# The head of a group-normalised convolution: pair 0 loaded in four transfers, its first upper half made in two operations, and a store placed ahead of a load

## The reference

```python
g = v.reshape(B_, G, C_ // G, H_, W_)          # G = 32 groups of two channels
m = mean(g, axis=(2, 3, 4)); s = var(g, axis=(2, 3, 4))
gn = ((g - m) / sqrt(s + 1e-5)).reshape(v.shape)
out = x + conv(gn, sign(W), padding 1)         # the forward value of the binarised weight is sign(W)
```

## Time and profile before

| | |
|---|---|
| median of 3 runs | 206.25 us (205.93 to 206.54) |
| the profiled execution, its own time | 206.47 us |
| its span | 204.7 us |
| TensorE matmul busy | 196.7 us, 96% of the span |
| weight loads, beside the matmuls | 165.3 us, 81% |
| VectorE busy | 149.0 us, 73% |
| ScalarE busy | 138.5 us, 68% |
| GpSimd busy | 134.8 us, 66% |
| HBM traffic | 25.84 MB read, 25.69 MB written, 252 GB/s over the span |

### The profile page before, as it was taken

How to read it: one execution, slowest core, us unless ns; L and a number is a source line. 1 busy time by engine, 2 the same in 40 slices (tenths; PEclk the granted TensorE clock), 3 DMA queues, 4 the chain that set the end, 5 groups by cost and what they waited for, 6 DMA issues and landing times.

```text
span 204.7 us, 10453 instructions
## 1 busy us (share of the span) xinstructions
PE 196.7 (96%) x4782; PEld 165.3 (81%) x4782; DVE 149.0 (73%) x320; ACT 138.5 (68%) x177; POOL 134.8 (66%) x86
## 2 busy tenths in 40 slices
PE   1999999999999999999999999999999999999993
PEld 0686978878899999989788787978788797878873
DVE  1894997976949496794949689594958859460955
ACT  3295969588593949769394976939496794939500
POOL 1059596939586793958578495858859585875900
PEclk9999999999999999999999999999999999999999
DMA  6949788887969788796979879697887969442464
GB/s 209 313 152 303 202 335 278 259 298 210 351 180 378 235 275 286 220 382 164 366 218 294 284 231 365 144 387 205 307 283 261 304 172 370 181 160 95 154 230 160
DMA packets 19116, 52.20 MB, mean 255 GB/s; under 512 B 2112, under 2 KB 4928, under 8 KB 19072
## 3 DMA queue, kind: packets, MB, share of 16 engines
q1 hardware_dynamic: 19072, 51.54, 74.9%
HBM read 25.84 MB, written 25.69 MB: 252 GB/s over the span
## 4 chain that ended last, share of the span: by engine, by line
PE 92%; DMA 3%; DVE 2%; SPq 1%; ACT 0%; issue 0%; DVEq 0%
PE psum L513 91%; DMA w_raw<-in_L_conv_W_dram 3%; DVE xbuf L466 2%; SPq L155 1%; PE psum L487 1%; ACT w_sign L290 0%; PE psum L497 0%; DVEq L56 0%
## 5 line engine op out<-in xcount | busy, mean ns | idle before, releaser
L236 POOL TENSOR_TENSOR los<-xnorm,his 128x840 f16<-128x840 f32 (+1 forms) x64 | 105.9, 1686 | 26.4 <-ACT his L274 15.8
L513 PE MATMUL psum<-los,w_taps 64*64 64x392 f16 (+1 forms) x2268 | 110.5, 325 | 0.0
L513 PE MATMUL psum<-his,w_taps 64*64 64x392 f16 x2268 | 110.2, 325 | 0.0
L513 PEld LDWEIGHTS psum<-his,w_taps 64*64 64x64 f16 x2268 | 81.9, 107 | 15.8 <-issue 0.4
L513 PEld LDWEIGHTS psum<-los,w_taps 64*64 64x64 f16 x2268 | 84.1, 107 | 13.0 <-POOL los L236 0.6
L388 DVE SCALAR_TENSOR_TENSOR xbuf<-psum,xbuf 128x784 f32<-128x784 f32 (+1 forms) x60 | 58.1, 969 | 40.8 <-PE psum L513 39.9
L339 DVE BATCH_NORM_STATS2 stats<-xbuf 128x6 f32<-128x448 f32 x112 | 64.0, 614 | 4.4 <-DMA xbuf<-in_x_dram 3.9
L266 ACT ACTIVATE xnorm<-xbuf,coef 128x784 f32<-128x784 f32 (+2 forms) x62 | 62.7, 1035 | 1.4 <-DVE coef L371 1.0
L274 ACT CAST his<-xnorm 128x784 f16<-128x784 f32 (+2 forms) x62 | 50.2, 835 | 0.3 <-issue 0.2
L242 POOL TENSOR_TENSOR xbuf<-moved,xbuf 128x784 f32<-128x784 f32 x15 | 27.9, 1863 | 32.9 <-ACT moved L283 32.9
L282 ACT ACTIVATE moved<-psum 64x784 f32<-64x784 f32 x15 | 12.3, 820 | 44.2 <-PE psum L513 44.2
(11 more groups left out here) (26 smaller groups left out, 21.8 us busy)
## 6 DMA issues: line engine op xcount, KB each, us to landing
out_dram<-xbuf SPq DMA_DIRECT2D x63, 392.0 KB, 4.7
xbuf<-in_x_dram SPq DMA_DIRECT2D x47, 448.0 KB, 4.4
xbuf<-in_x_dram SPq DMA_DIRECT2D x18, 224.0 KB, 4.9
out_dram<-xbuf SPq DMA_DIRECT2D x1, 224.0 KB, 2.2
out_dram<-xbuf SPq DMA_DIRECT2D x2, 84.0 KB, 1.8
w_raw<-in_L_conv_W_dram SPq DMA_DIRECT2D x1, 144.0 KB, 5.3
```

The costliest lines, as they stand in the source:

```text
L236: nc.gpsimd.tensor_tensor(rows(los[:, pair % HRING, :], a, b), rows(xnorm[:, pair % NRING, :], a, b), rows(his[:, pair % HRING, :], a, b), ...
L513: mm = pe.matmul(outs[:, a - n * BR:b - n * BR, left:right], w_taps[lanes, t, :], rows(half[lanes, slot, :], a + dy, b + dy)[:, :, left + ...
```

## The change

Pair 0 is loaded in four transfers of one, two, two and two of its seven pieces, in place of five of two, two, one, one, one. Its first upper part (15 rows) is made in two operations of 8 and 7 rows, each raising hi_first, and GpSimd's first los waits for both. In the first phase of pair 0 the taps of block 0 (the first two matmuls of a pass) run two taps ahead of those of block 1: after two half passes of block 0 alone TensorE waits for the second operation, goes on with both blocks, and ends with two half passes of block 1 alone. In SyncE's loop the store of a pair's first half stands ahead of the load that waits for the pair's fourth phase.

```diff
@@ -44,7 +44,7 @@
     SN = 8 * W
     NS = HW // SN
     PARTS = [range(0, 2), range(2, 4), range(4, 6), range(6, NS)]
-    PARTS0 = [range(0, 2), range(2, 4), range(4, 5), range(5, 6), range(6, NS)]
+    PARTS0 = [range(0, 1), range(1, 3), range(3, 5), range(5, NS)]
     assert PAIRS % XRING == 0 and (PAIRS - 1) % HRING == 0
 
 
@@ -191,8 +191,8 @@
             for phases in range(1, 4):
                 load_after(phases)
             for pair in range(PAIRS - 1):
+                store(pair, 0)
                 load_after(4 * pair + 4)
-                store(pair, 0)
                 load_after(4 * pair + 5)
                 store(pair, 1)
                 load_after(4 * pair + 6)
@@ -230,7 +230,7 @@
                 if pair == 0 and c < 2:
                     pool.wait_ge(xnorm_first, c + 1)
                 if pair == 0 and c == 0:
-                    pool.wait_ge(hi_first, 1)
+                    pool.wait_ge(hi_first, 2)
                 else:
                     pool.wait_ge(hi_ready, hi_done(pair, c))
                 nc.gpsimd.tensor_tensor(rows(los[:, pair % HRING, :], a, b), rows(xnorm[:, pair % NRING, :], a, b),
@@ -376,11 +376,12 @@
                 nc.vector.tensor_scalar(xnorm[:, 0, a * W:b * W], xbuf[:, 0, a * W:b * W],
                                         coef[:, 0, 0:1], coef[:, 0, 1:2], ALU.mult, ALU.add).then_inc(xnorm_first, 1)
 
+
             def hi_of_first():
-                a, b = CHUNKS[0]
                 dve.wait_ge(coef_ready, 1)
-                nc.vector.tensor_scalar(his[:, 0, a * W:b * W], xbuf[:, 0, a * W:b * W],
-                                        group[:, 0:1], coef[:, 0, 0:1], ALU.subtract, ALU.mult).then_inc(hi_first, 1)
+                for a, b in ((0, BR + 1), (BR + 1, CUTS[1])):
+                    nc.vector.tensor_scalar(his[:, 0, a * W:b * W], xbuf[:, 0, a * W:b * W],
+                                            group[:, 0:1], coef[:, 0, 0:1], ALU.subtract, ALU.mult).then_inc(hi_first, 1)
 
 
             def evacuate(pair, g, lanes, of, odd, done):
@@ -503,11 +504,12 @@
 
             ORDER = [4, 0, 2, 6, 8, 1, 3, 5, 7]
 
-            def products(slot, half, g, k, t, start, stop):
+            def products(slot, half, g, k, t, start, stop, parities=(0, 1)):
                 dy, dx = t // KW - 1, t % KW - 1
                 left, right = max(0, -dx), min(W, W - dx)
                 n0 = 4 * g + 2 * k
-                for lanes, cols, n in ((LOW, LOW, n0), (HIGH, HIGH, n0), (LOW, HIGH, n0 + 1), (HIGH, LOW, n0 + 1)):
+                tiles = ((LOW, LOW, n0), (HIGH, HIGH, n0), (LOW, HIGH, n0 + 1), (HIGH, LOW, n0 + 1))
+                for lanes, cols, n in tiles[2 * parities[0]:2 * parities[-1] + 2]:
                     a, b = max(n * BR, -dy), min((n + 1) * BR, H - dy)
                     outs = psum[cols, bank_of(n), 0:BN].rearrange("p (h w) -> p h w", w=W)
                     mm = pe.matmul(outs[:, a - n * BR:b - n * BR, left:right], w_taps[lanes, t, :],
@@ -551,10 +553,16 @@
                     if pair == 0 and g == 0:
 
                         pe.wait_ge(hi_first, 1)
-                        for i, t in enumerate(ORDER):
-                            if t == 1:
-                                pe.wait_ge(w_ready, 2)
-                            products(slot, his, 0, 0, t, i == 0, False)
+
+                        for i in range(TAPS + 2):
+                            if i < TAPS:
+                                if ORDER[i] == 1:
+                                    pe.wait_ge(w_ready, 2)
+                                products(slot, his, 0, 0, ORDER[i], i == 0, False, (0,))
+                            if i == 2:
+                                pe.wait_ge(hi_first, 2)
+                            if i >= 2:
+                                products(slot, his, 0, 0, ORDER[i - 2], i == 2, False, (1,))
                         pe.wait_ge(hi_ready, hi_done(0, 1))
                         phase(slot, 0, 1)
                         pe.wait_ge(lo_ready, lo_done(0, 0))
```

## The result

The changed kernel takes 208.3 us (median of 20 runs, 206.70 to 210.09) against 206.17 us (20 runs, 205.59 to 206.84) before: 2.1 us longer. The median lies outside the range that was given (205.7 to 207.6 us). Its direction is the one that was forecast, its size three times as large (2.1 against 0.65 us).

A forecast was written before the change was run, and what follows sets the result against it. TensorE's one long piece of 186.89 us was taken to bound the kernel, so only its start counts. Later statistics, the split and half passes, partly hidden, summed to +0.67 us: 206.25 + 0.67 = 206.9 us, range 205.7 to 207.6.

The forecast's parts named there:

- What bounds the kernel: One piece of 186.89 us of TensorE work; only how early the first block begins and whether it runs without holes counts.
- Term 1: VectorE's statistics of pair 0 end later, two pieces behind the last landing: +0.58 us, bounds -0.05 and +0.9 us.
- Term 2: The earlier first half of the upper part does not start TensorE's convolution sooner: no gain.
- Term 3: Splitting the first upper half in two operations delays the bias, normalised piece and GpSimd: +0.09 us, ends 0 and 0.15.
- The passes: Half passes of two matmuls lengthen the first 18 his passes on TensorE: +0.17 us, from a range of 0.17 to 0.33.
- Term 4: In SyncE's loop, putting the store ahead of the load does not hold the load: 0.
- rival D: TensorE's clock still low at the convolution's start after the pause behind the warm-up: 208 us, at most 208.7; chance 6%.
- A: The forecast itself, the start of the convolution block shifted later: 206.9 us, own range 206.6 to 207.3; chance 55%.

The follow-up runs named there:

- e1: The kernel before with only the four transfers of one, two, two and two pieces: 209.15 us, ratio 1.0135.
- e4: The changed kernel with 18 warm-up rounds in place of 14 ahead of the first transposes: 207.82 us, ratio 1.0075.
- e9: The changed kernel with its warm-up spread over the four landings and 9 rounds between the transposes in place of 6: 207.85 us, ratio 1.0063.
- e2: The kernel before with only the upper half in two operations and block 0 two taps ahead: 206.32 us, ratio 1.0008.
- e14: The changed kernel with pair 0 in six transfers of one, two, one, one, one, one piece and the warm-up spread over them: 206.27 us, ratio 0.9985.
- e3: The kernel before with only the store moved ahead of the load: 205.97 us, ratio 0.9999.
- e7: The changed kernel with 9 warm-up rounds between the two transposes in place of 6: 208.25 us, ratio 1.0075.
- e6: The changed kernel with the warm-up waiting for pair 0's second landing in place of the first: 207.84 us, ratio 1.0075.
- e8: The changed kernel with 18 warm-up rounds ahead of the first transposes and 9 between the transposes, in place of 14 and 6: 207.40 us, ratio 1.0056.
- e15: The kernel before with seven transfers of one piece, the warm-up spread over them and the store ahead of the load: 207.30 us, ratio 1.0036.
- e5: The kernel before with 10 warm-up rounds ahead of the first transposes in place of 14: 206.62 us, ratio 1.0007.
- e11: The kernel before with 10 warm-up rounds ahead of the first transposes and 3 between the transposes, in place of 14 and 6: 207.54 us, ratio 1.0055.
- e12: The kernel before with pair 0 in four transfers of two, two, two and one piece: 207.19 us, ratio 1.0014.

## Why the prediction was wrong

- **What bounds the kernel**: right. The long piece was 187.14 us after and 186.89 before; all that changed lies ahead of 17 us.
- **Term 1, statistics, +0.58 us**: in the profiled execution +0.35 us. The last landing came at 7.93 us and not 8.1, and two statistics took 1.15 us. Its mechanism stood in every profile with the four transfers, but its size scatters: the last statistics end at 9.1 us (after), 9.6 (e1), 9.4 (e4), 10.7 (e9) against 8.75 before. The bound of +0.9 us was too near: in e9 it is +2.0. I took the third landing as fixed by the bytes it closes; with two pieces in it, it came between 6.1 and 8.5 us. This is the second step that failed.
- **Term 2, the earlier half brings nothing**: right. It was there at 10.98 + 0.51 = 11.5 us, and TensorE's first weight load came at 11.61 us, right behind the last round. That load moved by 0.15 us only, though the deviation moved by 0.35: the copy behind it had waited for the first transposes as well, and came 0.20 us later (10.14 against 9.94 us). I had allowed it 0.05 us of slack.
- **Term 3, +0.09 us**: measured +0.19 us (0.82 against 0.63 us from start to start). The slope between 784 and 840 columns was carried too far: 448 and 392 columns take 0.514 and 0.479 us. Here the 0.16 us by the Trainium skill's fixed term (VectorE: DVE Perf Modes, the TRN2 errata) was the better number.
- **The passes, +0.17 us**: both his phases take 3.48 us from their first matmul where they took 3.18 in the same view, +0.30 us, close to the upper end of two passes; in e2 it is +0.15 us (3.33 us), in e14 +0.22 us. It costs next to nothing here, as GpSimd's piece is ready at the same time (12.85 + 2.17 = 15.02 us); e2 as a whole is at +0.1 us.
- **Term 4, the store, 0**: right. The two stores are issued from 22.28 us in place of 24.32, now ahead of the third load, which follows at 24.42 us; it was at 23.87 us, and moved as all of TensorE's work did (+0.55 us), so it is not held. e3's ratio is 0.9999.

```profile
18.44 3.32 SPq L165 DMA_DIRECT2D xbuf<-in_x_dram  x2
22.28 0.82 SPq L184 DMA_DIRECT2D out_dram<-xbuf  x2
```

- **The step that failed is rival D**, which the sum of 206.9 us put at nothing. Its mechanism was the one that decided, and its place was named: the pause between warm-up and transposes. It got 6%, and 13 of 20 runs have a low clock. Two readings were wrong in it. I let the warm-up start at 3.8 us and end at 8.6 us; it started at 3.40 us and was over at 7.94 us, so the idle time was 1.48 us and not the 0.7 us until 9.3 us. And I took the later shift of 0.5 us in ScalarE's chain for a shift only, when it opened a second idle stretch on TensorE of 0.49 us. The Trainium skill (TensorE: Matmul & The Clock Gate, Part 1) says the clock follows how busy the array has lately been; e7, where it fell under work after 2.1 us without a matmul, agrees.
- **That D's price came near is luck in part.** It said 208 us, at most 208.7; the runs with a low clock have 208.73 us. But it priced a clock that is still low when the convolution begins, on top of term 1's 0.58 us. In e1's profile the clock had risen before and fell again, that cost about 1.0 us and not 1.8, and the rest came from later statistics and an idle stretch at 55 us. With more or later warm-up and the four transfers left (e4, e6, e8, e9), the median is still 207.4 to 207.9 us: 0.5 to 1.0 us above the forecast. e9's profile shows late landings there, for which term 1's bound had no room; how much of the median they make, and how much a clock that rises late, stays open.
- **The likeliest case** (A, 206.9 us) is what the seven runs without a low clock show, 206.95 us. It was a minority of the runs. Three quarters of its 55% and D's 6% make 47%, not 48; nothing hangs on it.

## What to carry to other kernels

When an edit moves the signal that starts a warm-up, or the one that ends the pause behind it, cost the idle time of TensorE between them like an operation: here the terms of the sum made 0.67 us, and the runs with a low clock stand 1.8 us above the others. A profile is one execution, so look at the granted clock of every run before trusting it as the typical one. Place what the first statistics wait for in steps that VectorE can work off one by one, with the warm-up spread over the same landings: with six transfers (e14) that made the same edits harmless, with seven (e15) it did not.

## What the runs showed of the hardware that was not expected

- The granted clock fell to 0.50 while TensorE worked (e7, 10.7 us), after 2.14 us without a matmul that had ended at 9.97 us. With a first idle stretch of 1.63 us and 0.18 us behind it (e5's profile) no run's mean was under 0.995; with 1.36 and 0.67 us (e11's) three of twelve were.
- The same 14 warm-up rounds took 4.79 us (before), 4.54 us (changed kernel) and 3.95 us (e2), as TensorE became faster at another point of them or not at all.
- One of the sixteen parts of a transfer can land 1.2 to 2.3 us behind the other fifteen (e12: 7.54 against 6.36 us; e9: 8.48 against 6.20 us), and in e9 one part of each of the two transfers behind it was 1.6 us late as well. Seven small transfers did not prevent it (e15: 6.02 us, where eight parts had landed by 4.58 us).
- Passes with two matmuls of four are not free: two of them ahead and two behind, in place of two full ones, made the 18 passes of his 3.33 us (e2) to 3.48 us (changed kernel) long in place of 3.18; two full passes more would be 0.33 us.
